# The last layer of a two-layer transformer block, a ternary feed-forward with a depthwise convolution, rebuilt around pairs of channel tiles

## The reference, cut to what matters

```python
def act_quant(x):
    scale = 127.0 / jnp.clip(jnp.max(jnp.abs(x), axis=-1, keepdims=True), 1e-05)
    return jnp.clip(jnp.round(x * scale), -128, 127) / scale

def weight_quant(w):
    scale = 1.0 / jnp.clip(jnp.mean(jnp.abs(w)), 1e-05)
    return jnp.clip(jnp.round(w * scale), -1, 1) / scale

h = bit_linear(x, w1)                         # 512 -> 2048 channels, act_quant(x), weight_quant(w1)
h = depthwise_conv1d(h.transpose(0, 2, 1), conv_w, conv_b)   # 3 taps along the tokens, per channel
h = jax.nn.silu(h.transpose(0, 2, 1))
return bit_linear(h, w2)                      # act_quant needs the largest |h| of each token
x = x + jnp.tanh(g_ffn[1]) * that             # the last residual
```

## Time and profile before

| | |
|---|---|
| time, median of 3 runs | 2144.72 us (2134.03 to 2144.78) |
| profiled execution, its own time | 2152.16 us |
| span of its trace | 2150.5 us |
| busy over the span | PE 1645.3 us, DVE 1308.2, ACT 833.9, POOL 592.9, PEld 855.4 |
| start of the ternary layer's transfers | 1639.75 us |
| first reduction of step maxima, last one | 1707.5 us, 2106.4 us |
| end of the span | 2150.5 us |

### The profile page before, as it was taken

How to read it: one execution, slowest core, us unless ns; L and a number is a source line. 1 busy time by engine, 2 the same in 40 slices (tenths; PEclk the granted TensorE clock), 3 DMA queues, 4 the chain that set the end, 5 groups by cost and what they waited for, 6 DMA issues and landing times. The chain is left out here.

```text
span 2150.5 us, 24819 instructions
## 1 busy us (share of the span) xinstructions
PE 1645.3 (77%) x8769; PEld 855.4 (40%) x8799; DVE 1308.2 (61%) x2006; ACT 833.9 (39%) x1307; POOL 592.9 (28%) x600
## 2 busy tenths in 40 slices
PE   5788888872358879679999999999883476666663
PEld 4444444431125634355555555455331133332221
DVE  2578888874822433135546566564552688888996
ACT  3354444322813513044223232232201566656652
POOL 3132222110022200121111111111101877666661
PEclk9899999996678999879999999999996678778777
DMA  4012222126111335230120210200104111101111
GB/s 169 1 40 79 79 78 78 60 98 265 78 39 59 99 107 170 88 103 2 39 69 1 69 50 20 69 30 20 49 30 167 35 54 39 38 32 54 45 39 39
DMA packets 78738, 144.22 MB, mean 67 GB/s; under 512 B 13601, under 2 KB 22997, under 8 KB 78122
## 3 DMA queue, kind: packets, MB, share of 16 engines
q1 hardware_dynamic: 77674, 139.69, 19.1%
q0 software_dynamic: 960, 3.15, 0.5%
HBM read 99.79 MB, written 43.03 MB: 66 GB/s over the span
## 5 line engine op out<-in xcount | busy, mean ns | idle before, releaser
L558 PE MATMUL D_PJ<-D_wo,D_oT 128*128 128x512 f32 x512 | 229.2, 599 | 5.5 <-DVE D_res L695 3.8
L1656 POOL TENSOR_TENSOR E_cv<-E_cv,E_left 128x512 f32<-128x512 f32 x128 | 178.5, 1397 | 108.1 <-ACT E_left L1706 102.4
L1621 PE MATMUL E_HP<-E_xT,E_w1q 128*128 128x512 bf16 x491 | 157.0, 455 | 44.0 <-DVE E_hs L1790 38.1
L1701 ACT ACTIVATE E_cv<-E_hs,E_cb,E_cw 128x512 f32<-128x512 f32 x128 | 103.4, 808 | 134.0 <-DVE E_hs L1790 133.7
L514 ACT ACTIVATE D_probs<-D_SC 128x512 f32<-128x512 f32 x128 | 66.1, 603 | 228.5 <-PE D_SC L620 228.5
L1736 DVE SCALAR_TENSOR_TENSOR E_cv<-E_hs,E_cw,E_cv 128x512 f32<-128x512 f32 x128 | 109.6, 857 | 55.7 <-POOL E_cv L1656 55.6
L558 PEld LDWEIGHTS D_PJ<-D_wo,D_oT 128*128 128x128 f32 x512 | 94.6, 190 | 118.9 <-issue 107.3
L1580 PE MATMUL E_OP<-E_w2q,E_yb 128*128 128x512 bf16 x503 | 128.8, 401 | 15.6 <-ACT E_yb L1682 14.9
L558 PE MATMUL A_PJ<-A_wo,A_oT 128*128 128x512 f32 x256 | 129.1, 631 | 14.4 <-DVE A_q_low L744 10.2
L779 DVE TENSOR_TENSOR D_oT<-D_OB,D_rz 128x512 f32<-128x512 f32 x64 | 44.0, 688 | 139.4 <-PE D_OB L587 138.9
L418 POOL TENSOR_TENSOR D_rstd<-D_var,minus_half 128x1 f32<-128x1 f32 x32 | 17.5, 546 | 393.5 <-DVE D_var L701 393.5
(11 more groups left out here) (321 smaller groups left out, 3627.3 us busy)
## 6 DMA issues: line engine op xcount, KB each, us to landing
A_x<-in_x SPq DMA_DIRECT2D x8, 1024.0 KB, 5.3
A_res<-in_x SPq DMA_DIRECT2D x8, 1024.0 KB, 5.9
x_d<-A_res SPq DMA_DIRECT2D x8, 1024.0 KB, 4.3
xn_d<-A_xn SPq DMA_DIRECT2D x8, 1024.0 KB, 7.8
W_raw<-in_w1T SPq DMA_DIRECT2D x16, 512.0 KB, 4.5
W_raw<-in_w2T SPq DMA_DIRECT2D x16, 512.0 KB, 4.3
D_x<-x_d SPq DMA_DIRECT2D x8, 1024.0 KB
D_res<-x_d SPq DMA_DIRECT2D x8, 1024.0 KB, 6.5
```

The costliest lines, as they stand in the source:

```text
L558: mm = pe.matmul(PJ[:, :], oT[par][:, k, c * P:(c + 1) * P], wo[:, k, :], start=k == 0, stop=k == QT - 1)
L1621: mm = pe.matmul(HP[:, m % 2, :], w1q[:, k, m * P:(m + 1) * P], XT[par][:, k, 0:TILE], start=k == 0, stop=k == KD - 1)
L1656: pool.tensor_tensor(cv[m % NBUF][:, :], cv[m % NBUF][:, :], LP[m % 2][:, :], ALU.add).then_inc(t0, 1)
L1701: act.activation(cv[m % NBUF][:, :], hs[m % NBUF][:, 1:TILE + 1], ACT.Identity, bias=cb[:, m:m + 1], scale=cw[:, m, 1:2]).then_inc(cen, 1)
```

## The change

Only `ternary_layer` is rewritten. What it does:

- Channel tiles are taken in pairs (p = 0 to 7, `MP`), and the number i = 8n + p counts pairs. `HP` holds two pairs (four banks). DVE scales a pair in one instruction of 1024 columns; ACT's SiLU and POOL's adding work on 1024 columns.
- `cv` and `LP` are gone. ACT writes the left tap plus bias of both tiles straight into `Y`, and the centre tap of the odd tile into `U`; POOL makes the centre tap of the even tile, as a TENSOR_TENSOR with the tap broadcast, and adds `U` into `Y`. DVE adds the right taps in `Y`; SiLU works in place.
- The single reduction over a step is gone. For every pair PE turns the 8 blocks of 128x128 of `Y` (fp32) into `YT` (two banks), and DVE reduces 1024 columns to 4 per pair (`biggest(i)`). PE does pair i-5 after `project_in` of pair i, DVE pair i-4 ahead of `scale` of pair i.
- `TX` has no bank of its own any more: it lies in the bank of `SBK`, holds half a step's input, and is filled and emptied twice per step (PE at p = 1 and 3, ACT at p = 2 and 4). `OP` has one bank, not two.
- The halo columns of all 8 steps are made once at the start, so 64 small multiplications and a halo reduction per step go.
- The hardware loop is gone: all steps are written out. The last store is split in four.

```diff
-        HP, TX = pb("HP", [P, 2, TILE]), pb("TX", [P, KD, TILE], BF16)
-        AM, SBK, OP = pb("AM", [P, TILE]), pb("SB", [P, TILE]), pb("OP", [P, 2, TILE])
+        MP, NBUF, LAG, FOLD = MC // 2, 4, 2, 4
+        HP, YT = pb("HP", [P, 2, 2, TILE]), pb("YT", [P, SUB, 2, P])
+        SBK, OP = pb("SB", [P, TILE]), pb("OP", [P, TILE])
+        TX = SBK[:, :].bitcast(BF16).rearrange("p (k n) -> p k n", n=TILE)
-        AT = dict(biggest=3, turn_max=5, units=4, spread=6, quant=(6, 7, 8, 9), out=(9, 11, 13, 15), add=(10, 12, 14),
-                  turn=3, edges=7, halo=8)
+        QUANT, CAST, OUT, ADD = (4, 5, 6, 7), (5, 6, 7, 0), (7, 1, 3, 5), (6, 0, 2, 4)
...
+            def turn(n, half):
+                need(pe, x_te, 2 * n + half)
+                need(pe, q8, SUB * (n - 2))
+                pe.wait_ge(xq_in[n % 2], 16 * (n // 2 + 1))
...
+            def project_in(n, p):
+                i = MP * n + p
+                if p == 0:
+                    pe.wait_ge(x_te, 2 * n + 2)
+                need(pe, h_s, i - 1)
...
+            def project_out(n, c):
+                pe.wait_ge(qb, SUB * n + c + 1)
+                need(pe, o_ok, SUB * n + c)
...
+            def turn_y(i):
+                pe.wait_ge(sil, i + 1)
+                need(pe, amk, i)
...
             def spread(n):
                 pe.wait_ge(ru_ok, n + 1)
+                pe.wait_ge(x_te, 2 * min(n + 3, STEPS))
                 need(pe, q8, SUB * n)
...
+            for n in range(STEPS + 2):
+                for p in range(MP):
+                    i = MP * n + p
+                    if n < STEPS:
+                        project_in(n, p)
+                    if i == 0:
+                        edges()
+                        pe.wait_ge(w2_in, 16)
+                    if i == 1:
+                        pe.wait_ge(hh_ok, 1)
+                    if 0 <= i - FOLD - 1 < MP * STEPS:
+                        turn_y(i - FOLD - 1)
+                    if n + 1 < STEPS and p in (1, 3):
+                        turn(n + 1, p // 2)
+                    if 1 <= n <= STEPS and p == FOLD + 1:
                         spread(n - 1)
+                    if p in OUT:
+                        done = n - 1 if p == MP - 1 else n - 2
+                        if 0 <= done < STEPS:
+                            project_out(done, OUT.index(p))
...
+            for n in range(STEPS + 2):
+                for p in range(MP):
+                    i = MP * n + p
+                    if n < STEPS:
+                        products(n, p)
+                    if 0 <= i - LAG < MP * STEPS:
+                        silu(i - LAG)
+                    if p in CAST:
+                        s = n - 1 if p else n - 2
+                        if 0 <= s < STEPS:
+                            to_bf16(s, CAST.index(p))
+                    if n + 1 < STEPS and p in (2, 4):
+                        keep_xT(n + 1, p // 2 - 1)
...
+            def biggest(i):
+                dve.wait_ge(y_tr, i + 1)
+                if i % MP == 0:
+                    need(dve, a2_ok, i // MP)
+                dve.tensor_reduce(am[:, :, i % MP], YT[:, :, :, :].rearrange("p c e x -> p c (e x)"), AX.X, ALU.max,
+                                  apply_absolute_value=True).then_inc(amk, 1)
...
+            for n in range(STEPS + 2):
+                for p in range(MP):
+                    i = MP * n + p
+                    if 0 <= i - FOLD < MP * STEPS:
+                        biggest(i - FOLD)
+                    if n < STEPS:
+                        scale(n, p)
+                    if 0 <= i - LAG < MP * STEPS:
+                        right_taps(i - LAG)
+                    if 1 <= n <= STEPS:
+                        if p == FOLD - 1:
+                            units(n - 1)
+                        if p in QUANT:
+                            quantise(n - 1, QUANT.index(p))
+                    if p in ADD:
+                        done = n - 1 if p == ADD[0] else n - 2
+                        if 0 <= done < STEPS:
+                            add_out(done, ADD.index(p))
```

More of the change, by code:

```diff
@@ L1471, in ternary_layer @@
+        rsq, rsh, hh = sb("rs_q", [2 * STEPS, 1]), sb("rs_halo", [P, 2 * STEPS]), sb("hh", [P, MC, 2 * STEPS])
+        hs = [sb(f"hs{i}", [P, 2, TILE + 2]) for i in range(NBUF)]
+        U = [sb(f"centre{i}", [P, 2, TILE]) for i in range(2)]
         Y = [sb(f"y{i}", [P, MC, TILE]) for i in range(2)]
         y8, yb = sb("y8", [P, MC, TILE], I8), sb("yb", [P, MC, TILE], BF16)
-        am, a2, un, ru, f2 = sb("am", [P, TILE]), sb("a2", [P, SUB]), sb("unit", [P, SUB]), sb("ru", [P, SUB]), sb("f2", [P, SUB])
+        am = sb("am", [P, SUB, MP])
@@ new lines, in store @@
+            def store(n):
+                if n < STEPS - 1:
+                    sp.wait_ge(o_ok, SUB * (n + 1))
+                    sp.dma_start(out_dr[n % 2, n // 2], R[n % 2][:, :, :]).then_inc(stored[n % 2], 16)
+                else:
+                    for c in range(SUB):
+                        sp.wait_ge(o_ok, SUB * n + c + 1)
+                        sp.dma_start(out_dr[n % 2, n // 2, :, c], R[n % 2][:, c, :]).then_inc(stored[n % 2], 16)
+            load_rows(0)
+            for b in range(NB):
+                for at, x, r in ((b * LAPS, left, rs_l), (STEPS + b * LAPS, right, rs_r)):
+                    sp.dma_start(HQ[at:at + LAPS, :], x[b]).then_inc(hq_in, 16)
+                    sp.dma_start(rsq[at:at + LAPS, :], r[b], allow_slow_non_contiguous=True).then_inc(hq_in, 16)
@@ L1627, in _ @@
-            run_steps(pe, step, 1, front=2)
-            turn_max(STEPS - 1, STEPS)
-            spread(STEPS - 1)
-            for c in range(SUB):
-                for half in range(2):
-                    project_out(STEPS - 1, c, half)
+            for half in range(2):
+                turn(0, half)
+            pe.wait_ge(hq_in, 16 * 4 * NB)
+            for k in range(KD):
+                mm = pe.transpose(ht[:, k, :], HQ[:, k * P:(k + 1) * P], identb[0:2 * STEPS, 0:2 * STEPS])
+            pe.transpose(hr, rsq[:, 0:1].to_broadcast([2 * STEPS, P]), ident[0:2 * STEPS, 0:2 * STEPS]).then_inc(h_tr, 1)
@@ new lines, in right_taps @@
+            def right_taps(i):
+                n, p = divmod(i, MP)
+                dve.wait_ge(t0, i + 1)
+                for e in range(2):
+                    m = 2 * p + e
+                    dve.scalar_tensor_tensor(out=Y[n % 2][:, m, :], in0=hs[i % NBUF][:, e, 2:TILE + 2],
+                                             scalar=cw[:, m, 2:3], in1=Y[n % 2][:, m, :], op0=ALU.mult, op1=ALU.add)\
+                       .then_inc(t2, 1)
+            def biggest(i):
[4 more added lines that the diff above has]
+                                  apply_absolute_value=True).then_inc(amk, 1)
@@ L1805, in _ @@
-            run_steps(dve, step, 1, front=2)
-            for m in range(MC - LAG, MC):
-                right_tap(STEPS - 1, m)
-            add_out(STEPS - 2, LAPS - 1, 0, SUB - 1)
-            biggest(STEPS - 1, 1)
-            units(STEPS - 1)
-            dve.wait_ge(f_ok, STEPS)
-            for c in range(SUB):
-                quantise(STEPS - 1, 1, c)
-            for c in range(SUB):
-                add_out(STEPS - 1, LAPS - 1, 1, c)
+            dve.wait_ge(hb_mm, 1)
+            dve.wait_ge(xh_ok, 2)
```

349 lines of the change are left out of this document (128 added, 221 removed).

## The result

The changed kernel takes 2213.24 us (median of 4 runs, 2205.77 to 2218.74) against 2141.52 before (4 runs, 2134.03 to 2144.78): ratio 1.0323, 95% interval 1.0292 to 1.0353. It is 3.2% slower; 2220 had been predicted.

A forecast was written before the change was run, and what follows sets the result against it. DVE was taken to bound the old 57.6 us step. Waits of 63.2 plus 8 gave 71 per step; with start and tail the end came 75 us above before: 2220 us, 3.5% slower, range 2158 to 2290.

The forecast's parts named there:

- The price of the removed reduction: DVE's large reduction per 512-token step: the change removes 13.9 us of it.
- Sums of work: Work per engine and step: DVE 42, PE 37, ACT 33, POOL 31 to 41 us; order decides, not the sum.
- rival 1: Sums decide if PE's waits for ACT are hidden: step near 46, about 2060 us, faster; chance 0.14.
- The round of waits: Middle step followed through DVE, PE and ACT hand-overs at full clock: four pieces summing to 63.2 us, 5.6 more than before.
- The 8 for clock and taps: Added per step for PE's lost clock, with taps waiting for POOL (0 to 5) put into it: 8 us, so 71.
- Two taps: DVE's two right taps of a pair, priced at 1.32 us together.
- The start of the layer: From layer start through step 0: pair 1 of step 1 at 1720, against 1722 before, so nothing won.
- The signs I had named: PE idle near 6 us at two places, DVE idle ahead of `biggest`, step 63 to 75, clock near or below 0.77.
- signs of being wrong: L1750 rarely idle and step under 57; a `biggest` over 1.8; taps well over 1 on average; DVE waiting for POOL.
- Rival 2: No change: waits cost 5 to 6 us less per step and the clock holds, 2135 to 2155 us; chance 0.06.
- Rival 3: PE stays at half clock throughout: 94 us per step, about 2390 us; chance 0.06.
- Rival 4: Taps and POOL collide at every tap: 16 x 1.0, step 79, about 2275 us; counted with the forecast.

The follow-up runs named there:

- e8: The kernel before, with its large reduction over 2 of the 16 channel tiles, so 14 are left out of the maxima: 2032.7 us, ratio 0.949.
- e3: The changed kernel with ACT's input copies at pairs 1 and 3 and PE's turning ahead of the next projection: 2097.7 us, ratio 0.978.
- e9: The changed kernel with copies at pairs 0 and 2, casts at pairs 4 to 7, turning first, both centre taps on ACT: 2039.1 us, ratio 0.951.
- e1: The changed kernel with ACT's copies of the turned input at pairs 1 and 3, not 2 and 4: 2118.9 us, ratio 0.988.
- e2: The changed kernel with PE turning the maxima's input ahead of the next projection, copies left late: 2162.4 us, ratio 1.008.
- e6: The changed kernel in its own order, with ACT making the even tile's centre tap too, instead of POOL: 2218.7 us, ratio 1.035.
- e4: The changed kernel with 20 unused multiplications in PE ahead of each wait for ACT in steps 2 to 6: 2208.7 us, ratio 1.029.
- e12: e9 with the even centre tap back on POOL: 2074.8 us, ratio 0.968.

## Why the prediction was right, step by step

**The price of the removed reduction** (13.9 us of a step, all of it exposed) was right: e8 gave back 13.5. **Sums of work** were right in that they decide nothing here: 42 us for DVE was the forecast without collisions, and DVE was busy 49.3 of e3's 54.5. With nearly every wait gone (e9) the step is 44.1, which is rival 1, "the sums decide", with its 46. The rival had the right end point and a condition, either hand-over moved; the change doesn't meet it. e1 moves both, and no run moves one alone.

**The round of waits**, the step on which all rested, is what happened. The four pieces, from the ends of scaling 1, 3, 5, 7 and 1 (1912.19, 1933.66, 1956.37, 1970.50, 1983.95):

| piece | predicted, full clock | measured | what the rest is |
|---|---|---|---|
| pair 1 to 3 | 18.35 | 21.47 | projection 3.50 for 1.89; 1.3 in turning and `project_out` |
| pair 3 to 5 | 18.5 | 22.71 | L1763 2.11; turning and `project_out` 6.6 for 4.1 |
| pair 5 to 7 | 13.65 | 14.13 | DVE's second taps wait for POOL; DVE's own work, put at 10.2 and covered, takes 11.8 and sets the end |
| pair 7 to 1 | 12.65 | 13.45 | the same |
| step | 63.2, and 8 on top: 71 | 71.8 | |

The link that carries it, from the end of DVE's scaling to the end of ACT's copy, was predicted as 0.1 + 2.05 + 0.95 + 1.0 = 4.1 and measured 4.10 (1919.10 to 1923.20). e1 shows that this link is the cause: moved, 94 us go. Most of that cost comes about because the turning is queued behind it: e2 keeps the waits and takes back 51.

**The 8 for clock and taps** held as a sum (8.6) and roughly in its parts: 5.4 of lower clock, worked out from the durations in the table (1.6 + 1.3 + 2.5), and 3.2 of meetings with POOL. It was not placed rightly. I had the clock lost behind the two waits; a fifth of the whole excess is in the projection ahead of the first one, behind a gap of 2.45 us that I had put under "shorter gaps" at 2 for all of them. And a tap was what I feared for POOL, where the dearest single meeting is the units' small L1763: 0.26 us by itself (e9's row of that instruction), 1.88 on average here, since POOL's addition was running.

**`biggest`** at 1.15, the lower bound, was right: 1.22, and 1.14 start to start (1916.74 to 1917.88). **Two taps** at 1.32 were not: 2.18 where POOL's centre tap is ready, which is nearly always (60 of 64 pairs).

**The start of the layer** was mis-sized. I put pair 1 of step 1 at 1720; it ended at 1702.64. Of these 17 us, 11.5 are the unchanged layers ahead, which in this execution ended earlier, and 6 are mine: behind E_cw I had allowed 67.2 and it took 61.3, since PE, put at half clock in step 0, was granted 0.80 in 1642 to 1702.6, and the first projection ran ahead of the wait for the second weights. From there to the last scaling I had 64 + 355 + 39 = 458, and it took 465.3 (65.1, 359.0, 41.2). The tail was 47 and took 45.5. So the layer's length came to 572.1 against 572.2 by the sum, with errors of -6, +7 and -1.5 that cancel: that the layer came out to the microsecond is luck. Of the 7 us under 2220, 3.2 are the median of before that I had added the 75 to (2144.72, and 2141.52 with the fourth run); the rest is within the scatter of the layers ahead.

**The signs I had named** were there but one: PE idles 6.55 and 8.27 where I put near 6 (the trace gives ACT's E_xT as releaser for the first alone), DVE idles ahead of L1750 for E_YT, the step lies in 63 to 75. The clock was to be near or below 0.77 and is 0.82: from 1720 us on PE stands still for more than 2 us 41 times, against 17 before, but never for longer than 8.3, where before it stood for 14.32 in a step. Of the signs of being wrong one came: taps over 1 on average (1.14).

**Rival 2** (no change) fell with the waits' size. **Rival 3** (half clock throughout, 2390) fell by the granted clock, 0.82 in the layer, and full by the time of the projection behind each wait (1.89 us at 1928.50 and at 1951.21). The turnings that were to keep it down did not where PE had no long waits: e9 has 64 of them in a step and a clock of 0.94. **Rival 4** (every tap collides) is half true: the second tap of each of a step's 8 pairs waits 0.77, but most have slack behind them, as e6 shows.

The Trainium skill (SBUF — State Buffer, Who interferes with whom) says that a VectorE instruction with two SBUF inputs contends with a GpSimd one that reads SBUF, and that the one which starts first holds the port to its end. The trace agrees: with POOL's tap gone and the order kept (e6) 62 of 64 pairs of taps take 1.4, with it 60 of 64 take 2.18.

**Left open**: the clock's exact share. e4 filled the gap only in part, and the 5.4 us are worked out from durations, not shown by a run that changes the clock and nothing else. I also have not separated e9's gain over e12 into fewer meetings and better clock (0.90 and 0.94 from 1640 us to the end).

## What to carry to other kernels

Before removing a reduction from the busiest engine, write down who waits for whom over one round: here three engines got less work and PE's share of the span stayed at 77%, and the layer grew by 74 us, because an in-order engine had its next producer queued behind a hand-over from a third engine. Place the instruction that frees a buffer a stage ahead of the one that wants it; it took two edited lines here and was worth 94 us. Then take one wait at a time: an edit that is worth nothing now (e6) can be worth 36 us when the waits ahead of it are gone, so try it again behind each step.
